# Router logits of a mixture-of-experts stage with the gate weights stationary instead of the tokens

## The reference

```
x = x + attn_ref(_layernorm(x), ...)          # LN, qkv, head attention, wo, LN, gelu MLP
x = x + ffn_ref(_layernorm(x), ...)

def ffn_ref(x, gate_w, w_up, w_down, sg_gate, sg_up, sg_down):
    logits = xf @ gate_w.T                     # 8192 x 8
    topk_logits, topk_idx = top_k(logits, 2)
    topk_w = softmax(topk_logits)
    out = sum over experts e of comb[:, e] * (silu(xf @ wg[e].T) * (xf @ wu[e].T) @ w_down[e].T)
    shared = silu(xf @ sg_gate.T) * (xf @ sg_up.T) @ sg_down.T
    return shared + out
```

## Time and profile before

| what | value |
|---|---|
| median of 3 runs | 1974.54 us (1974.48 to 1976.22) |
| time of the profiled execution | 1976.3 us |
| its span, first to last instruction | 1974.5 us |
| mean granted TensorE clock | 0.937 of full speed |
| one block in the loop, `stage_b` to `stage_b` | 77.6 us |

### The profile page before, as it was taken

How to read it: one execution, slowest core, us unless ns; L and a number is a source line. 1 busy time by engine, 2 the same in 40 slices (tenths; PEclk the granted TensorE clock), 3 DMA queues, 4 the chain that set the end, 5 groups by cost and what they waited for, 6 DMA issues and landing times.

```text
span 1974.5 us, 28277 instructions
## 1 busy us (share of the span) xinstructions
PE 1772.7 (90%) x6885; PEld 1148.7 (58%) x6886; DVE 1435.4 (73%) x2625; ACT 812.8 (41%) x1526; POOL 1260.4 (64%) x756
## 2 busy tenths in 40 slices
PE   3489898898998898988989988879999999999997
PEld 2255565565555555655655556456666666666665
DVE  7888999998999999989989999334444444444443
ACT  3245445355464554453554644422222222222222
POOL 5876898888878988988788789512333333333333
PEclk8689898898898998988988989879999999999999
DMA  4112110110110101101101101013333333333333
GB/s 158 74 44 107 44 43 22 43 43 21 43 35 29 43 11 43 43 21 43 43 21 43 35 19 44 33 46 62 54 59 58 54 59 56 56 59 56 56 54 48
DMA packets 75753, 94.90 MB, mean 48 GB/s; under 512 B 8400, under 2 KB 69712, under 8 KB 74448
## 3 DMA queue, kind: packets, MB, share of 16 engines
q0 software_dynamic: 25584, 34.75, 10.0%
q1 hardware_dynamic: 50144, 59.85, 9.5%
HBM read 49.18 MB, written 45.38 MB: 48 GB/s over the span
## 4 chain that ended last, share of the span: by engine, by line
PE 46%; DMA 26%; DVE 9%; issue 8%; POOL 5%; ACT 4%; POOLq 1%; ACTq 0%; DVEq 0%
DMA out_rows<-prod_pool,prod 26%; PE p_b L1161 17%; PE p_b L1209 11%; PE p_b L1240 6%; PE p_q L1133 5%; PE p_v L1133 3%; DVE prod L813 2%; POOL prod_pool L440 2%; DVE kvT L796 2%; DVE chosen L902 1%; PE p_b L1147 1%; ACT L607 1%; PE p_b L1232 1%; POOL prod_pool L514 1%; ACT bT L596 1%
## 5 line engine op out<-in xcount | busy, mean ns | idle before, releaser
L543 POOL DMA_INDIRECT out_rows<-prod_pool,prod x135 | 209.7, 1553 | 432.7 <-DMA out_rows<-prod_pool,prod 396.5
L440 POOL TENSOR_TENSOR prod_pool<-prod_pool 128x544 f32<-128x544 f32 (+4 forms) x240 | 399.7, 1666 | 18.8
L1209 PE MATMUL p_b<-bT,fc_sb 128*128 128x512 f32 x512 | 226.2, 600 | 12.1 <-ACT bT L639 12.1
L1161 PE MATMUL p_b<-proj_sb,hid 128*128 128x256 f32 x1024 | 230.5, 379 | 0.0
L796 DVE TENSOR_REDUCE kvT<-prod 128x128 f32<-128x2048 f32 x96 | 219.5, 2286 | 2.7
L788 DVE TENSOR_TENSOR prod<-p_q,v_dve 128x4096 f32<-128x4096 f32 x48 | 211.9, 4414 | 0.0
L1240 PE MATMUL p_b<-bT,sgup_sb 128*128 128x512 f32 x384 | 206.5, 695 | 0.0
L1161 PEld LDWEIGHTS p_b<-proj_sb,hid 128*128 128x128 f32 x1024 | 189.7, 190 | 27.7 <-issue 0.5
L1313 PE MATMUL p_b<-exp_sb,prod 128*128 x810 | 197.3, 380 | 0.8 <-DVE prod L1095 0.8
L1297 PE MATMUL p_q<-exp_sb,prod 128*128 x544 | 186.9, 487 | 0.6 <-ACT prod L694 0.6
L1297 PE MATMUL p_b<-exp_sb,prod 128*128 x536 | 185.1, 488 | 0.3 <-issue 0.3
(11 more groups left out here) (158 smaller groups left out, 2961.0 us busy)
## 6 DMA issues: line engine op xcount, KB each, us to landing
prod<-rows_sorted SPq DMA_DIRECT2D x135, 130.0 KB, 2.1
exp_sb<-in_experts SPq DMA_DIRECT2D x8, 1152.0 KB, 10.3
xin<-in_x SPq DMA_DIRECT2D x16, 512.0 KB, 3.4
xres<-in_x SPq DMA_DIRECT2D x16, 512.0 KB, 3.5
out_rows<-x SPq DMA_DIRECT2D x16, 512.0 KB, 3.1
out_rows<-prod_pool,prod POOLq DMA_INDIRECT x135, 3.8
rows_sorted<-rows,slot POOLq DMA_INDIRECT x128
rows_sorted<-pad_row SPq DMA_DIRECT2D x1, 1040.0 KB, 5.0
```

The costliest lines, as they stand in the source:

```text
L440: done(g.tensor_tensor(prod_pool[:, at:at + n * w], prod_pool[:, at:at + n * w], prod_pool[:, at + n * w:at + 2 * n * w], ALU.add))
L543: pool.indirect_dma_start(out=out[:, :], out_offset=bass.IndirectOffsetOnAxis(ap=tok_i[j], axis=0), in_=yg[j], in_offset=None, compute_op= ...
L1161: ins = t_.matmul(o, src[:, k, t * P:(t + 1) * P], w[:, k, :], start=k == 0, stop=bias_at is None and k == chunks - 1)
L1209: ins = t_.matmul(bnk[:], fc_sb[:, k, f * P:(f + 1) * P], bT[:, k, :], start=k == 0, stop=k == KC - 1)
```

## The change

`gate_sb` gets 32 columns (8 experts and 24 of zeros). The logits are computed transposed, `[32, 512]` in `p_b1[0:32]`, by two products with the gate weights stationary and 512 tokens moving. ACT copies them to `logT`, 32 partitions of `hid`'s last chunk. After the first shared product (n = 0), PE multiplies each 128-token slice of `logT` (stationary, 32 partitions) by an 8-column piece of the identity, which puts the logits back, tokens by partition, where `choose` reads them in `p_b1`. `logits_psum` is raised there.

```
+GATE_W = 32
...
-        gate_sb = sb("gate_sb", [P, KC, EXPERTS])
+        gate_sb = sb("gate_sb", [P, KC, GATE_W])
...
+        logT = hid[0:GATE_W, FCH - 1, :]
...
                     take_pair(c, (p_b2, p_b3), x3T_psum, x3T_ready)
+                    wait(act, logT_psum, c)
+                    a.activation(logT, p_b1[0:GATE_W, :], ACT.Copy).then_inc(logT_ready, 1)
                     table(ACT.Silu)
...
                     wait(pe, x3T_ready, KC * c)
-                    for t in range(TPB):
-                        for k in range(KC):
-                            at = LOGITS + t * EXPERTS
-                            ins = t_.matmul(p_b1[:, at:at + EXPERTS], bT[:, k, t * P:(t + 1) * P],
-                                            gate_sb[:, k, :], start=k == 0, stop=k == KC - 1)
-                    ins.then_inc(logits_psum, 1)
+                    for k in range(KC):
+                        ins = t_.matmul(p_b1[0:GATE_W, :], gate_sb[:, k, :], bT[:, k, :],
+                                        start=k == 0, stop=k == KC - 1)
+                    ins.then_inc(logT_psum, 1)
                     for n in range(2 * HCH):
+                        if n == 1:
+                            wait(pe, logT_ready, c)
+                            for t in range(TPB):
+                                at = LOGITS + t * EXPERTS
+                                ins = t_.matmul(p_b1[:, at:at + EXPERTS], logT[:, t * P:(t + 1) * P],
+                                                ident[0:GATE_W, 0:EXPERTS], start=True, stop=True)
+                            ins.then_inc(logits_psum, 1)
```

More of the change, by code:

```diff
@@ L248, in build @@
         x3T_ready = sem("x3T_ready")
+        logT_psum = sem("logT_psum")
+        logT_ready = sem("logT_ready")
         logits_psum = sem("logits_psum")
@@ L1378 @@
         "proj_w": rows_of(get("attn_proj_w")),
-        "gate_w": rows_of(get("ffn_gate_w").T),
+        "gate_w": rows_of(np.pad(get("ffn_gate_w").T, ((0, 0), (0, GATE_W - EXPERTS)))),
         "sg_up": rows_of(np.concatenate([get("ffn_sg_gate"), get("ffn_sg_up")], axis=0).T),
```

## The result

The changed kernel takes 1990.4 us (median of 4 runs, 1988.22 to 1994.91) against 1974.51 of the kernel before beside it: ratio 1.0082, 95% interval 1.0063 to 1.0101. It is slower by 15.9 us, where 12 were forecast (1986, range 1975 to 2016). The profiled execution took 1994.91, the longest of the four, and has a span of 1993.1 us. T is again the start of the logits; in block 5 it is 460.61.

A forecast was written before the change was run, and what follows sets the result against it. A ring through POOL's list, `chosen` on DVE, `ranks` and PE was taken to bound the kernel. Later `choose` costs 0.89 us in each of 13 blocks, 11.6 us in all: median 1986 us, range 1975 to 2016.

The forecast's parts named there:

- the sum: Blocks 2 to 14 each lose 0.89 us, 11.6 us in all; blocks 1, 15 and 16 left at nothing.
- What bounds the kernel: Ring of `gate_shared`, POOL's list, `chosen`, `ranks`, qkv and shared products; a delay of `ranks` lengthens a block in full.
- The logits on PE: Old logits matmuls of 3.58 us replaced by four wide ones, 3.45 us at the low clock: gain 0.1.
- The clock: PE's clock rises earlier, 3.4 to 5.9 us after T, since the wide logits products count like others.
- Rival one: PE's clock does not rise earlier; 2.8 us a block on average, 37 us: 2011 us; chance 0.27.
- The small products: Eight loads and eight matmuls on PE behind n = 0, 0.9 us at the high clock, 1.8 at the low.
- that rival: PE's loads do not follow the clock, so the small products take 1.8 us; 24 us slower: 1998; chance 0.04.
- ACT's copy: Copy of the logits on ACT, at most 0.60 us, half hidden and done before n = 0 ends: cost nothing.
- POOL's boundaries: `gap` issued by T+7.96 costs 0, in POOL's L450 1.42, after T+8.8 2.26 us; 0.89 a block taken.
- `onehot` slips in: On DVE, `onehot` gets in before POOL's L458, 0.02 us ahead; 0 to 4 us, 1976 us; chance 0.15.
- The falls of the clock: PE idling 2 to 3 us ahead of `ranks` may let the clock fall once or twice; only in the range.
- PE the bound, the other side: PE, not `chosen`, decides when `ranks` starts; earlier n = 2 makes it 19 us faster, 1956 us; chance 0.08.

The follow-up runs named there:

- experiment 2: Kernel before, with the first `onehot` in PSUM so that `chosen` reads only one SBUF operand: 1960.1 us, ratio 0.9936.
- 1: Kernel before, with the signal of the logits raised one and a half shared products later, PE's work unchanged: 2019.56 us, ratio 1.0234.
- 5: Changed kernel, with the fourth shared product (n = 3) moved in front of `ranks`: 1958.82 us, ratio 0.9925.
- 3b: Changed kernel, with expert numbers, first `onehot` and a copy of the second logit in PSUM, freeing every operation of `choose`: 1953.56 us, ratio 0.9894.
- experiment 4: Changed kernel, with the four small products before the first shared product (n = 0) instead of behind it: 1982.85 us, ratio 1.0049.
- experiment 6: `gap` issued behind `chosen`: in the changed kernel 1984.18 us, ratio 1.0058; in the kernel before 1964.36 us, ratio 0.9949.

## Why the prediction was right, and which of its terms were off

The mechanism was right and the number close, but the closeness is partly luck. In the profile the loop grew by 23.0 us, twice the 11.6 of the sum. The stretch behind it, which the sum holds constant, gave 4.0 back, and the median execution lies below the profiled one.

*What bounds the kernel.* Right: the hold of `choose` behind POOL (experiment 2), the full passing on of a delay of `ranks` (1 and 5).

*The logits on PE.* 3.55 us to the start of n = 0, where the sum had 3.45 and the kernel before 3.44. The gain of 0.1 in the sum came from setting 3.58, the length of the old products to their end, beside 3.45, a spacing of starts. Start to start the old ones took 3.44, so nothing was to be gained, and 0.1 was lost.

*The clock.* The chosen case held: in blocks 2 to 14 the rise came at T+3.7 to 5.5, against T+3.4 to 5.9. The 24 columns of zeros did not keep it from rising; in 3b it came as early as T+2.7, before any of the shared products. Rival one falls.

*The small products.* The loads of L1245, 32 partitions and 128 columns, start 0.11 apart at the high clock (0.96 for 8, less 0.19 of the last):

```profile
466.60 0.96 PEld L1245 LDWEIGHTS p_b<-ident,hid 32*128 32x128 f32 x8 [0.76 <-issue]
```

In experiment 4 the same eight products took 1.87 us at the low clock, so the loads follow the clock, as in the earlier trace rows, and that rival falls too. The Trainium skill, "TensorE: Matmul & The Clock Gate", section "LDWEIGHTS (loading the stationary operand)", gives a load as its columns over 1.2 GHz, with one formula for both clocks; for 128 columns that is an estimate of 0.11 us. The trace agrees at the high clock (0.11) and not at the low one (0.21 in the earlier trace rows); the measurement decides.

*ACT's copy.* 0.59 for 32 partitions, as long as for 128 (0.60 in the earlier trace rows), and hidden:

```profile
464.27 0.59 ACT L669 ACTIVATE hid<-p_b 32x512 f32<-32x512 f32 x1 [3.71 <-PE p_b L1237]
```

*POOL's boundaries: the mis-sized term.* I gave four cases equal weight, two at no cost, and corrected the mean to 0.89 a block. Measured: MAX8 at T+6.7 to 7.6 where I had 6.4 to 7.6, so `gap` was issued at T+8.0 to 8.7 and never before the bound of T+7.96. In every block MAX8 is 0.2 later than the sum gives for the rise as measured; 0.10 of it is the logits, the rest lies between the start of n = 0 and the small products. By the sum, blocks 2, 6, 9 and 14, with rises at T+3.7 to 4.4, would still have passed in time. Twelve blocks fell into the class "issued in L450". In block 2 `gap` was issued 0.05 before the halving ended and passed at once, but the cast behind it, 0.71 us long, was held until L455 ended. I had not counted the cast among the held operations, and `chosen` came as late as in the others. Eleven blocks cost 1.1 to 1.4, and in two (3 and 11) `chosen` slipped in between L463 and the halving: mean 14.9/13 = 1.15. The class of 2.26 did not occur.

*`onehot` slips in.* Half right, and it cost as forecast all the same: the first did slip in, with its lead of 0.02 in block 5 and in eight more of blocks 2 to 14, and the second was held. The Trainium skill, "SBUF — State Buffer", section "SBUF: two separate sides", lets the one that starts first keep the shared pair for the whole instruction. The trace agrees for the first and shows the rest: the second `onehot` had to get in anew, and did not. To a hundredth of a us the shown starts do not decide: in blocks 3 and 11 `chosen` got in although its start is shown 0.01 behind that of the halving.

*The falls of the clock.* "Once or twice" were four, 6.9 us. This term I had left in the range instead of the sum. The idle stretches were about as forecast, mostly 2.0 to 3.1 us. The 23.0 of the loop are then 14.9 (forecast 11.6), 6.9 (forecast nothing), 0.2 of the outer blocks (nothing) and 1.0 without a name.

*PE the bound, the other side.* PE's work did end earlier, T+10.2 to 11.1 by the ends shown (forecast 9.6 to 10.9), but `chosen` decided. The 19 us that this rival priced are real once the hold is gone: 20.7 in 3b (1974.29 less 1953.56). Freeing `chosen` alone, with the old logits, gave 12.2 (1972.26 less 1960.1).

## What to carry to other kernels

Ask of an engine that looks slow on a tiny operation what the other engine was doing when it ended: an end that follows another's by 0.05 us in every block points to a hold, and moving one of the two SBUF inputs to PSUM tests it. Under a hold a small delay can cost a whole step of the other engine's list, not its own length. A producer that brings PE forward but signals later can lose more than it saved, and the idle stretch it makes on PE can cost a second time through the clock. Before such a change is given up, free the consumer: here 3b turns a loss of 15.9 us into a gain of 20.7.

## What the runs showed of the hardware that I had not expected

A cast from SBUF to SBUF with a single operand (8 elements a partition, uint32 to float32) is held by POOL's tensor_tensor too, 0.98 us in the row of experiment 6; written to PSUM in 3b it took 0.17 us, while the same cast to SBUF behind it was held up to 1.90. Of two DVE operations issued back to back, one can get in 0.02 us ahead of a POOL instruction and the other wait for nearly all of it (block 5 of the changed kernel). After products with 32 stationary columns, 24 of them zero, the clock rose at T+2.7 to 5.7 in 3b. With eight narrow products and 0.68 us of idle time behind them, the rise came at T+12.2 at worst (experiment 4).
